# Transposing the normalised context without its column of sums, in a cross-attention block

## The reference

```
xq  = layer_norm(x, qn_w, qn_b)
ctx = layer_norm(context, cn_w, cn_b)
q   = (xq @ q_w).reshape(B, N, H, D)
k, v = (ctx @ kv_w) split, each (B, M, H, D)
attn = softmax(where(mask, -max, q k^T * scale))
x   = x + (attn @ v).reshape(B, N, C) @ proj_w + proj_b
h   = layer_norm(x, n2_w, n2_b)
out = x + gelu(h @ fc1_w + fc1_b) @ fc2_w + fc2_b
```

## Time and profile before

| what | value |
| --- | --- |
| median of 3 timed runs | 887.91 us (887.74 to 892.45) |
| profiled execution, its own time | 891.24 us |
| its span | 889.4 us |
| PE busy | 799.8 us, 90% |
| DVE busy | 570.2 us, 64% |
| ACT busy | 558.6 us, 63% |
| POOL busy | 341.5 us, 38% |
| mean granted clock of PE | 0.954 of full |

### The profile page before, as it was taken

One profiled execution on the slowest core, in us unless ns is written; L12 is line 12 of the kernel. 1 busy time (PEld: TensorE's weight loads), 2 busy tenths in 40 slices (PEclk: granted clock), 3 DMA queues, 4 the chain that ended last, 5 costly groups with the idle time before them and its releaser, 6 DMA issues.

```text
span 889.4 us, 17043 instructions
## 1 busy us (share of the span) xinstructions
PE 799.8 (90%) x5637; PEld 645.0 (73%) x5637; DVE 570.2 (64%) x1238; ACT 558.6 (63%) x765; POOL 341.5 (38%) x312
## 2 busy tenths in 40 slices
PE   4329499999999999999999999999999999999998
PEld 3327376878787777878787877878787877778587
DVE  4433857768585867678585867677585858665241
ACT  2406566676767766666767677666767677676532
POOL 2010244343526253342526263443436262433324
PEclk9858689999999999999999999999999999999699
DMA  6582836739393847658393947567493938457000
GB/s 193 127 115 82 114 55 155 116 111 138 122 127 101 147 87 156 107 136 110 124 144 97 137 97 147 94 149 107 135 125 120 125 99 144 83 124 118 1 24 24
DMA packets 89446, 100.47 MB, mean 113 GB/s; under 512 B 9028, under 2 KB 63544, under 8 KB 89400
## 3 DMA queue, kind: packets, MB, share of 16 engines
q1 hardware_dynamic: 89088, 99.81, 59.1%
q10 hardware_dynamic: 328, 0.27, 0.2%
HBM read 69.22 MB, written 30.83 MB: 112 GB/s over the span
## 4 chain that ended last, share of the span: by engine, by line
PE 61%; issue 12%; DVE 9%; POOL 7%; ACT 2%; POOLq 0%; DVEq 0%; ACTq 0%
PE F L834 20%; PE A L834 9%; PE F L947 6%; PE A L914 5%; PE F L949 5%; PE F L948 5%; PE ST L905 4%; POOL oT_lo L427 3%; DVE shift L655 2%; PE ST L887 2%; PE A L930 2%; POOL xin L416 2%; POOL xin L421 2%; PE A L887 1%; DVE shift L648 1%
## 5 line engine op out<-in xcount | busy, mean ns | idle before, releaser
L433 POOL TENSOR_TENSOR g_lo<-g_f,g_hi 128x512 fp32r<-128x512 f32 x128 | 166.5, 1305 | 209.2 <-ACT g_hi L535 194.2
L501 ACT ACTIVATE probs<-ST 78x512 f32<-78x512 f32 x256 | 137.5, 588 | 45.4 <-PE ST L905 44.4
L947 PE MATMUL F<-w_hi,g_hi 128*128 128x256 f32 x512 | 159.0, 311 | 0.7 <-POOL g_lo L433 0.7
L948 PE MATMUL F<-w_lo,g_hi 128*128 128x256 f32 x512 | 145.8, 285 | 0.0
L949 PE MATMUL F<-w_hi,g_lo 128*128 128x256 f32 x512 | 145.6, 284 | 0.0
L533 ACT ACTIVATE g_f<-F,bias 128x512 f32<-128x512 f32 x128 | 88.1, 688 | 73.7 <-PE F L834 44.2
L947 PEld LDWEIGHTS F<-w_hi,g_hi 128*128 128x128 f32 x512 | 98.5, 192 | 40.3 <-issue 39.4
L521 ACT ACTIVATE QM<-mask_u 77x2048 fp32r<-77x2048 uint8 x64 | 116.8, 1897 | 0.0
L834 PE MATMUL F<-xT_hi,w_hi 128*128 128x512 f32 x256 | 108.6, 424 | 1.7 <-DVE xT_lo L580 1.7
L905 PE MATMUL ST<-QM,KM 127*78 127x256 f32 x512 | 91.1, 294 | 14.0 <-DMA QM<-sd 11.9
L834 PE MATMUL F<-xT_hi,w_lo 128*128 128x512 f32 x256 | 101.2, 395 | 0.0
(11 more groups left out here) (141 smaller groups left out, 1661.9 us busy)
## 6 DMA issues: line engine op xcount, KB each, us to landing
QM<-qd SPq DMA_DIRECT2D x48, 512.0 KB, 14.7
xa<-in_x SPq DMA_DIRECT2D x16, 512.0 KB, 4.0
qd<-q_hi SPq DMA_DIRECT2D x32, 256.0 KB, 2.1
qd<-q_lo SPq DMA_DIRECT2D x32, 256.0 KB, 2.1
xin<-in_x SPq DMA_DIRECT2D x16, 512.0 KB, 5.2
out<-xin SPq DMA_DIRECT2D x32, 256.0 KB, 6.0
QR<-qd SPq DMA_DIRECT2D x16, 480.0 KB, 5.3
KM<-kd SPq DMA_DIRECT2D x48, 156.0 KB, 6.9
```

What stands on the lines that cost most here:

```text
L433: pool.tensor_tensor(g_lo[:, k], g_f[k % 2][:], g_hi[:, k].bitcast(F32), ALU.subtract).then_inc(g_lo_done, 1)
L501: act.activation(probs[:, quad % NSLOT, 2 * (p % 2):2 * (p % 2) + 2], ST[p % 2][0:MX].rearrange("p (h n) -> p h n", n=N), ACT.Exp, scale=S ...
L947: pe.matmul(dst, g_hi[:, k, tok], w2_hi[:, k], start=(k == 0), stop=False)
L948: pe.matmul(dst, g_hi[:, k, tok], w2_lo[:, k], start=False, stop=False)
```

## The change

The product with `isum` becomes a transpose by PE with the 77 by 77 corner of the plain identity `ident`. It writes 77 of the 78 columns of each block. The sums are now made by DVE: at the head of `cT_split` a reduction adds the 77 columns of each of the four blocks and writes the result into the 78th, in the same bank. The copy that makes cT_hi waits for it. `isum` and the three POOL instructions that made it are gone, and `CONSTS` falls from 20 to 17.

```
@@ GpSimd, startup
             pool.memset(ident[:], 0.0).then_inc(consts, 1)
-            pool.memset(isum[:], 0.0).then_inc(consts, 1)
             pool.memset(pat_m[:], 0.0).then_inc(consts, 1)
...
-            pool.affine_select(out=isum[:], in_=isum[:], compare_op=ALU.not_equal, fill=1.0, base=0,
-                               pattern=[[-1, MX]], channel_multiplier=1).then_inc(consts, 1)
...
-            pool.wait_ge(consts, 18)
-            pool.memset(isum[:, M:MX], 1.0).then_inc(consts, 1)
+            pool.wait_ge(consts, 16)
@@ VectorE
             def cT_split(j):
                 dve.wait_ge(cT_mm, j + 1)
                 dve.wait_ge(shift_stored, 16 * j)
+                per_batch = cT_cols.rearrange("p k (b m) -> p (k b) m", m=MX)
+                dve.tensor_reduce(per_batch[:, :, M:MX], per_batch[:, :, 0:M], X, ALU.add).then_inc(c_sum_done, 1)
+                dve.wait_ge(c_sum_done, j + 1)
                 dve.tensor_copy(cT_hi[:], cT_cols).then_inc(cT_hi_done, 1)
                 dve.wait_ge(cT_hi_done, j + 1)
                 low(cT_lo[:], cT_cols, cT_hi[:]).then_inc(cT_lo_done, 1)
@@ TensorE
             def cT(j):
                 pe.wait_ge(cn_done, NB * (j + 1))
                 for k in range(KC):
                     for b in range(NB):
-                        last = pe.matmul(cT_cols[:, k, b * MX:(b + 1) * MX], cn[:, b, k * P:(k + 1) * P], isum[:],
-                                         start=True, stop=True)
+                        last = pe.transpose(cT_cols[:, k, b * MX:b * MX + M], cn[:, b, k * P:(k + 1) * P], ident[0:M, 0:M])
                 last.then_inc(cT_mm, 1)
```

More of the change, by code:

```diff
@@ L67, in xattn_block @@
         ident = sb("ident", [P, P])
-        isum = sb("isum", [M, MX])
         neg_half = sb("neg_half", [P, TT + NB])
@@ L165, in xattn_block @@
         cT_mm = sem("cT_mm")
+        c_sum_done = sem("c_sum_done")
         cT_hi_done = sem("cT_hi_done")
@@ L376, in _ @@
             pool.memset(V[:], 1.0).then_inc(consts, 1)
-            pool.wait_ge(consts, 11)
+            pool.wait_ge(consts, 10)
             pool.affine_select(out=ident[:], in_=ident[:], compare_op=ALU.not_equal, fill=1.0, base=0,
                                pattern=[[-1, P]], channel_multiplier=1).then_inc(consts, 1)
-            pool.affine_select(out=isum[:], in_=isum[:], compare_op=ALU.not_equal, fill=1.0, base=0,
-                               pattern=[[-1, MX]], channel_multiplier=1).then_inc(consts, 1)
             pool.affine_select(out=pat_m[:, 0, 0:M], in_=pat_m[:, 0, 0:M], compare_op=ALU.not_equal, fill=-BIG, base=0,
@@ L1094, in _ @@
                     fc2(PAIRS - 1, t, k)
-CONSTS = 20
+CONSTS = 17
 QKV_READY = 2 + 2 + 2
```

## The result

The changed kernel took 883.89 us (median of 7 runs, 880.3 to 887.05) against 887.91 (7 runs, 886.42 to 892.45): a ratio of 0.9948 with a 95% interval of 0.9924 to 0.9972. The profiled execution has a span of 881.9 us, against 889.4.

What follows compares the result with a forecast made beforehand. PE, busy 90%, was the main load, but ACT's table load and exps set its pace in full-clock bodies. Startup -0.5, body 0 -0.5 and late q_proj +0.1 gave -0.9 us: 887.91 to 887.0, range 884.5 to 891.5.

Steps and rivals of the forecast that it cites:

- middle, new form: Full-clock bodies: q_proj 0.01 us late in each of 7 even bodies, called a loss of 0.1 us.
- I cost this gain at nothing: Full-clock bodies: shorter cT frees 0.43 us of PE each, all lost waiting for ACT's exp 0.
- Rival 3: Full-clock bodies: fc2 products and scores move up with cT, 6.0 us plus 1.0 at the start, 881; chance 5%.
- The DVE step: Ahead of the cT split: a reduction adds 0.48 to 0.50 us per cT, bounds 0.45 and 0.65.
- The slack: Full-clock bodies: DVE delay covered before k_proj by 0.19 us, before q_proj by 0.09; k_lo's 0.41 wait absorbs most.
- Body 0: Low-clock cT: 0.81 us off the path, 0.4 if the clock rises when it did; counted 0.5, bounds 0.4 and 0.81.
- My sentence from the Trainium skill: Under rival 1: full clock does not engage for transposes, making a fallen clock likely; the trace spoke against a strong reading.
- The startup: Fewer GpSimd constants 0.4, shorter cT(0) 0.8, DVE step -0.5: 0.7 us gained, counted 0.5, bounds 0 and 1.3.
- Rivals 1 and 2: Rival 1: clock falls in every body, about 929, 6%. Rival 2: DVE step twice its row, 892.4, 4%.
- My range: Whole kernel: 884.5 to 891.5 us, widened for clock rises and the earlier runs' 4.7 us spread.
- the forecast case: Whole kernel: forecast 887.0 us, given 85%, with its own bounds 885.8 and 889.0.

Runs made afterwards that it cites:

- e5: Kernel before with the new form for pairs 0 and 1 alone, isum and tiles in place; 885.46 us, against 887.18 for the kernel before beside it.
- e10: e5 plus e7's heavy filling of the last body; 885.36 us, 1.7 below e7.
- e16: e13 with DVE's reduction added and the products with isum kept; costs 1.6 us, 0.8 of it in the middle.
- e7: Kernel before with heavy filling: 16, 12, 6 and 6 useless PE products in the last body; 887.03 us.
- e8: Changed kernel with the same heavy filling of the last body as e7; 883.43 us.
- e13: Kernel before with light filling: 12, 4, 2 and 2 useless PE products in the last body; 3.1 us from e12, own median not given.
- e12: Changed kernel with light filling: 12, 4, 2 and 2 useless PE products of 256 columns in the last body; 880.55 us.
- e15: Changed kernel with isum still allocated in its old place, plus light filling; new form worth 2.1 us against e13, own median not given.
- e6: Kernel before with the new form for pairs 2 to 15 only, isum and tiles in place; 885.02 us, against 887.18 for the kernel before beside it.
- the square: Light-filled kernels with old or new form, isum's tile in place or moved/removed, e12 as fourth corner; layout worth 1.3 and 1.0 us, new form 2.1 and 1.8.
- e9: e7 with the tile isum allocated last, so later tiles lie 312 bytes lower; 884.76 us, 2.3 below e7.
- e4: Kernel before with the tile isum allocated last, so later tiles lie 312 bytes lower, same instructions; 887.25 us.
- e3: Changed kernel with the tile isum allocated again but unused, so later tiles lie where they did before; 882.71 us.

## Why the prediction was wrong

Two of its steps were too small, and one term was missing. By the profiles, as means over all kernels that have the part in question:

```
part                                    forecast   measured   from
start to first scores of body 0         -0.5       -1.0       8 profiles at 66.3 to 67.8, mean 67.0; 7 at 65.2 to 66.8, mean 66.0
body 0, first scores to projection      -0.5       -1.8       the table above
projection of body 0 to cT of pair 2     0          0.0       9 and 9 profiles, 30.9 both
middle, new form                        +0.1       +0.2 to 0.4  643.8 to 644.2; 642.9 to 643.1
middle, layout                          none       -0.9 to 1.1  643.8 to 642.9; 644.2 to 643.1
sum                                     -0.9       -3.5
```

The first row leaves out e5, e10 and e16, which mix the two forms in the startup. The sum looks like the 3.6 us between e7 and e8 and the 3.1 between e13 and e12, but it holds 0.7 us of late rises in body 0, which those medians hardly have. Without the three late profiles, body 0 is at -1.1 and the sum at -2.8; that leaves 0.3 to 0.8 us of the medians unplaced, about their own error. The 4.0 between the first two medians also holds the end of the run with its low clock, between none and 20.5 us long in the profiles; against the 3.6 it is 0.4 more, within the scatter.

**"I cost this gain at nothing" in the full-clock bodies: right.** The 0.58 us that PE saves between cT and xT goes into the wait for exp 0. Rival 3 did not occur there; k_proj stands where it stood, 3.04 behind cT. The step erred only in its price, 0.58 for 0.43, since a transpose of 77 rows follows the next in some 0.07 us.

**The DVE step: right in kind and price.** 0.47 with 0.03 behind it. The slack that I worked out from the earlier trace rows held from body 2 on: with the tiles in place, two bodies take 99.0 to 99.1 us both in e15 and in e13. (In e6 and e16, q_proj comes 0.02 to 0.05 us late in the even bodies from 6 on, and 0.15 in body 4.) What I missed is body 1. There the reduction starts 1.67 us behind cT, not 1.31, because the copy of g_hi ahead of it takes 1.30 and not 0.94, and PE waits for cT_lo:

```profile
130.30 1.30 DVE L704 CAST g_hi<-g_f 128x512 fp32r<-128x512 f32 x1 [0.75 <-ACT g_f L529]
131.52 0.47 DVE L611 TENSOR_REDUCE A<-A 128x4 f32<-128x308 f32 x1
...
133.08 0.19 PEld L833 LDWEIGHTS A<-cT_hi,kvw_hi 128*128 128x128 f32 x1 [0.16 <-DVE cT_lo L576]
...
135.72 0.19 PEld L833 LDWEIGHTS A<-xT_hi,qw_hi 128*128 128x128 f32 x1 [0.51 <-DVE xT_lo L576]
```

q_proj comes 0.3 late in this one body: by e15 against e13, 0.27 of the 0.43 us that the new form costs in the middle. I had read bodies 7 and 8 and taken them for all fourteen.

**Body 0: the step that failed most.** I counted 0.5 with bounds of 0.4 and 0.81, on the thought that the clock rises when it rises, or at best with the work. The work saved is more than I had, and that is only a part of it:

```profile
67.31 0.71 PE L841 MATMUL A<-ident,cn 77*128 77x77 f32 x4
67.82 1.91 PE L847 MATMUL A<-ident,xa 128*128 128x128 f32 x8
68.06 0.49 DVE L611 TENSOR_REDUCE A<-A 128x4 f32<-128x308 f32 x1 [13.08 <-PE A L841]
...
69.38 0.99 PE L903 MATMUL ST<-QM,KM 127*78 127x256 f32 x3
```

From cT to xT it is 0.51 us and not 1.62, so 1.1 saved where I had halved it to 0.81. I then took most of that back for a clock that rises at the same moment as before. It doesn't: leaving the late ones out, it rises 6.2 us behind the first scores as a mean of six profiles with the old form, and 5.1 as a mean of nine with the new one, so the rise moved by what the work moved, and the whole 1.1 us stayed (33.4 to 32.3 for the stretch). On top there is the late rise at about 11 us, which cost body 0 a further 2 us in 3 of 9 profiles with the old form and was not seen in 9 with the new one. One profile of the kernel before could not tell me that this place has two outcomes. That the new form makes the late one rarer is not shown: if both forms had the same odds, all three late ones of 18 profiles would fall among the nine old ones by luck in 1 of 10 cases. My sentence from the Trainium skill (TensorE: Matmul & The Clock Gate, Part 4: PE-mode transpose), that the full clock does not engage for transposes, pointed the wrong way here: with more transposes and fewer products, the rise came no later.

**The startup: mis-sized.** 1.0 gained where I had 0.5, inside my bounds of 0 to 1.3. cT(0) starts 0.3 sooner (12.01), and its transposes take 0.78 instead of 1.99.

**The layout: left out.** Nothing in my sum is about the tiles behind isum. It is worth 0.9 to 1.1 us in the middle by the trace and 1.0 to 1.3 by the medians of the square. Why the lower addresses are quicker for PE is open; I tried no other shift. The 2.3 us of e9 and the nothing of e4 are both further from that than I can explain but by scatter and, for e4, by its end.

**Rivals 1 and 2.** The clock stays full through the middle, and the DVE step is not twice its row. The runs' spread I had put at 4.7 us from three runs; the kernel before spans 882.4 to 892.5 over all of them. My range was cut to the forecast case and its first profile.

## What to carry to other kernels

- Before costing an edit that removes a tile, ask what lies behind it: moving the others can be worth as much as the edit (here some 1.0 of 3.1 us). Keep the tile allocated in an experiment to separate the two.
- Time saved on PE ahead of a wait for another engine was worth nothing at full clock, but the same edit in a stretch at low clock, with no such wait behind it, saved double the time (1.1 us for 0.58), and the rise of the clock came forward with it. Read the odd bodies (first, second, last) by themselves; here they held most of the gain and the one real loss.
- Where runs scatter more than the effect, find the place that scatters in a few profiles and remove it from both kernels; some idle-time products in the last body took the standard deviation from 2 us to about 1, and done lightly they took 3 to 4 us off either kernel, as much as the change itself. A run's mean granted clock also tells in which of its outcomes it was, without a profile of it.

## What the runs showed of the hardware that I had not expected

- The low clock in the last body of one and the same kind of program lasted 0, 6.8, 10.2, 13.7 or 20.5 us in different executions, with PE busy nearly throughout. It began 0.9 to 2.6 us after the end of a wait of PE's of 1.5 us for ACT, when PE had gone on with scores and attention; in e6's profile the same wait of 1.50 us was followed by no low clock. By the timed runs the odds differ between kernels (7 of 11 runs of e3 without it, none of 127 of the kernel before), and no run shows why. Twenty products put into PE's waits there, 12, 4, 2 and 2 of them, kept the clock at full in all five profiles that had them.
- The same dense products on PE took 8.61 us or 8.54 us, depending on whether their operands' tiles lay 312 bytes higher or lower in SBUF.
- A float32 transpose of 77 rows takes 0.229 us in its row and follows the next after some 0.07 us at full clock; the float32 product of the same operand that it replaces takes two passes of 0.106.
